# Cross attention's mask as a table that VectorE adds to the scores, in place of a TensorE matmul, on one core

## The reference

```python
kv_c = kv @ W_kvc;  q_c = q @ W_dq                     # q = layernorm(x), kv = ctx_2048 (16, 1601, 256)
q_nope, q_rope = heads(q_c @ W_uq), rope(heads(q_c @ W_qr))        # 16 heads of 128, of 64
k_nope, v, k_rope = heads(kv_c @ W_uk), heads(kv_c @ W_uv), rope(kv_c @ W_kr)
scores = (q_nope . k_nope + q_rope . k_rope) / sqrt(192)
good = (k_ids <= seg_id) & (k_ids >= seg_id - 8)       # seg_id: one number per query token, 0 to 127
attn = softmax(where(good, scores, -1e30))             # over the 1601 keys
x = x + (attn @ v) @ W_o
```

## Time and profile before

| | us |
|---|---|
| median of 3 runs | 519.15 |
| lowest, highest | 518.19, 522.25 |
| the profiled execution: its time | 518.47 |
| the profiled execution: its span | 516.7 |
| PE busy | 499.3 (97%) |
| PEld busy | 363.5 (70%) |
| DVE busy | 249.6 (48%) |
| ACT busy | 185.2 (36%) |

### The profile page before, as it was taken

How to read it: one execution, slowest core, us unless ns; L and a number is a source line. 1 busy time by engine, 2 the same in 40 slices (tenths; PEclk the granted TensorE clock), 3 DMA queues, 4 the chain that set the end, 5 groups by cost and what they waited for, 6 DMA issues and landing times.

```text
span 516.7 us, 10575 instructions
## 1 busy us (share of the span) xinstructions
PE 499.3 (97%) x3878; PEld 363.5 (70%) x3878; DVE 249.6 (48%) x549; ACT 185.2 (36%) x534; POOL 60.3 (12%) x71
## 2 busy tenths in 40 slices
PE   8699999999999999997999998999999999999997
PEld 7476777777877788885798885555555555556886
DVE  2565876876766668987553221222222222222334
ACT  2157567566566444444411111112112112121110
POOL 2000000000000122132006500000000000000650
PEclk9799999999999999999999999999999999999999
DMA  9800000000991009400523162777877877852241
GB/s 289 321 22 1 20 22 1 19 20 15 362 410 48 2 17 408 189 0 1 209 98 126 70 220 90 269 264 279 306 270 283 310 261 291 301 210 82 80 125 41
DMA packets 24455, 82.05 MB, mean 159 GB/s; under 512 B 2880, under 2 KB 16512, under 8 KB 20320
## 3 DMA queue, kind: packets, MB, share of 16 engines
q1 hardware_dynamic: 21536, 75.93, 40.3%
q0 software_dynamic: 1536, 4.20, 2.6%
q10 hardware_dynamic: 1344, 1.38, 0.8%
HBM read 73.10 MB, written 8.39 MB: 158 GB/s over the span
## 4 chain that ended last, share of the span: by engine, by line
PE 88%; DVE 6%; issue 3%; ACT 2%; POOL 0%; DVEq 0%; ACTq 0%; POOLq 0%
PE ps L1808 17%; PE ps L1721 12%; PE ps L1317 12%; PE ps L1832 9%; PE ps L1733 6%; PE ps L1396 5%; PE ps L1346 5%; PE ps L1365 5%; PE ps L1488 3%; PE ps L1384 3%; ACT w_routed L1096 1%; PE ps L1322 1%; PE ps L1498 1%; PE ps L1677 1%; PE ps L1338 1%
## 5 line engine op out<-in xcount | busy, mean ns | idle before, releaser
L1808 PE MATMUL ps<-w_routed,xnT 128*64 x320 | 93.8, 436 | 1.6 <-DVE x_sb L967 1.6
L1721 PE MATMUL ps<-xT_all,w_shared 128*128 128x256 f32 x320 | 75.7, 380 | 0.0
L1808 PEld LDWEIGHTS ps<-w_routed,xnT 128*64 128x64 f32 x320 | 42.0, 137 | 38.4 <-issue 27.2
L1721 PEld LDWEIGHTS ps<-xT_all,w_shared 128*128 128x128 f32 x320 | 60.3, 190 | 8.4 <-issue 0.4
L1096 ACT ACTIVATE w_routed<-ps,neg_top 128x128 f32<-128x128 f32 x128 | 45.1, 379 | 15.8 <-DVE neg_top L637 15.8
L1317 PEld LDWEIGHTS ps<-consts_a,w_routed 128*128 128x128 f32 x336 | 38.8, 145 | 15.2 <-issue 12.1
L1317 PE MATMUL ps<-consts_a,w_routed 128*128 128x128 f32 x336 | 46.2, 283 | 2.4 <-DVE x_sb L565 1.4
L1832 PE MATMUL ps<-w_routed,hidT 128*64 x200 | 47.4, 384 | 0.0
L1808 PE MATMUL ps<-w_shared,xnT 128*64 128x384 f32 (+1 forms) x160 | 46.9, 436 | 0.0
L1808 PE MATMUL ps<-x_up,xnT 128*64 128x384 f32 (+1 forms) x160 | 46.9, 436 | 0.0
L1286 ACT COPY hidT<-ps 128x384 f32<-128x384 f32 x20 | 9.6, 479 | 100.7 <-PE ps L1317 100.7
(11 more groups left out here) (181 smaller groups left out, 870.6 us busy)
## 6 DMA issues: line engine op xcount, KB each, us to landing
w_routed<-in_w_routed SPq DMA_DIRECT2D x8, 1920.0 KB, 14.4
x_up<-in_w_routed SPq DMA_DIRECT2D x10, 1280.0 KB, 5.9
w_shared<-in_w_routed SPq DMA_DIRECT2D x10, 1280.0 KB, 6.1
b_down<-in_w_routed SPq DMA_DIRECT2D x10, 640.0 KB, 5.7
w_shared<-in_w_routed SPq DMA_DIRECT2D x10, 640.0 KB, 5.4
w_shared<-in_w_shared SPq DMA_DIRECT2D x1, 3840.0 KB, 11.7
w_shared<-in_w_uvo SPq DMA_DIRECT2D x1, 2560.0 KB, 15.4
x_slots<-sil SPq DMA_DIRECT2D x16, 160.0 KB, 2.1
```

The lines of the kernel that those rows point to most:

```text
L1721: last = pe.matmul(ps[:, UP_BANK[m], half_ * D:(half_ + 1) * D].rearrange("p (n t) -> p n t", n=2), w_shared[:, j, at:at + P], xT_all[:, i ...
L1808: last = pe.matmul(ps[rows, b, 0:hi - lo], xnT[:, k, rows], w, start=k == 0, stop=k == KT - 1)
```

## The change

In the setup, behind the first tile's queries, TensorE runs four matmuls of `sel` with the mask of four tiles each (512 columns, banks 4 to 7), and ScalarE copies each result as bf16 into a table `spread` of 128 x (8 tiles, 2 sequences, 128 keys), which lies in `b_down`, unused until the experts. In each tile the mask's four matmuls go, and a bank's score matmuls each start afresh. VectorE adds the table's row block, repeated over the four head pairs, to the scores in PSUM and writes them to `Pb` in SBUF (with a `link`), and takes the minimum from there. ScalarE's exponentials read `Pb` in place of PSUM, in place. The general path keeps its matmul and waits for the table.

```diff
+        spread = b_down[:, 0:NT * TB * P // 2].bitcast(BF16).rearrange("p (n b t) -> p n b t", n=NT, b=TB)
...
@@ general
+                eng.wait_ge(spread_done, 2 * TB)
...
@@ vector
-            def maxima(i, b):
+            def maxima(i, b, link_):
                 s = scores_at(b)
                 for g in range(2):
                     n = slice(4 * g, 4 * g + 4)
                     dve.wait_ge(s_ps, 2 * TB * i + 2 * b + g + 1)
-                    dve.tensor_reduce(neg_top[:, b, n], s[:, n], AX.X, ALU.min).then_inc(top_ready, 1)
+                    link_(dve.tensor_tensor(Pb[:, b, n], s[:, n], spread[:, i, b, :].unsqueeze(1).to_broadcast([P, 4, P]), ALU.add))
+                    dve.tensor_reduce(neg_top[:, b, n], Pb[:, b, n], AX.X, ALU.min).then_inc(top_ready, 1)
...
+            dve.wait_ge(spread_done, 2 * TB)
             body(0, link, False, True)
             body(1, link, True, True)
             base = steps[0]
-            K = 8
+            K = 12
...
@@ scalar
             def exps(i, b, groups=(0, 1)):
-                s = ps[:, 4 + 2 * b:6 + 2 * b, :].rearrange("p r (h t) -> p (r h) t", t=P)
                 for g in groups:
                     act.wait_ge(top_ready, 2 * TB * i + 2 * b + g + 1)
                     for n in range(4 * g, 4 * g + 4):
-                        last = act.activation(Pb[:, b, n, :], s[:, n, :], ACT.Exp, scale=-1.0,
+                        last = act.activation(Pb[:, b, n, :], Pb[:, b, n, :], ACT.Exp, scale=-1.0,
                                               bias=neg_top[:, b, n:n + 1], accum_out=sums[:, b, n:n + 1])
...
             lat_out(0)
+            for n in range(2 * TB):
+                act.wait_ge(spread_ps, n + 1)
+                act.copy(spread[:, n // TB * NT // 2:(n // TB + 1) * NT // 2, n % TB, :],
+                         ps[:, 4 + n, :].rearrange("p (n t) -> p n t", t=P)).then_inc(spread_done, 1)
...
@@ tensor
-            def scores_work(b, half_, window):
+            def scores_work(b, half_, window=None):
                 at = ps[:, 4 + 2 * b + half_, :]
-                pe.matmul(at.rearrange("p (n k) -> p n k", k=P), sel[:, b, :], window.unsqueeze(1).to_broadcast([P, 4, P]),
-                          start=True, stop=False)
+                if window is not None:
+                    pe.matmul(at.rearrange("p (n k) -> p n k", k=P), sel[:, b, :], window.unsqueeze(1).to_broadcast([P, 4, P]),
+                              start=True, stop=False)
                 for n in range(4):
                     h = 2 * (4 * half_ + n)
-                    last = pe.matmul(at[:, n * P:(n + 1) * P], QT[:, b, h:h + 2, :], KTb[:, b, :], start=False, stop=n == 3)
+                    last = pe.matmul(at[:, n * P:(n + 1) * P], QT[:, b, h:h + 2, :], KTb[:, b, :], start=window is None,
+                                     stop=window is None or n == 3)
...
             y_rope(0)
+            pe.wait_ge(win_ready, 1)
+            pe.wait_ge(far_ready, 1)
+            for n in range(2 * TB):
+                pe.matmul(ps[:, 4 + n, :].rearrange("p (n t) -> p n t", t=P), sel[:, n % TB, :],
+                          win[:, n // TB * NT // 2:(n // TB + 1) * NT // 2, :], start=True, stop=True).then_inc(spread_ps, 1)
...
-            pe.wait_ge(win_ready, 1)
+            pe.wait_ge(spread_done, 2 * TB)
             body(0, False)
```

More of the change, by code:

```diff
@@ L282, in build @@
             yrope_ps yrope_used qrope krope kT_ps kT_done qt_lo_ps qt_lo qt_hi_ps qt_hi kvx
-            s_ps top_ready exp_done p_done pt_ps pt_done ut_ps ut_done proj_ps x2_done ones_set
+            s_ps top_ready exp_done spread_ps spread_done p_done pt_ps pt_done ut_ps ut_done proj_ps x2_done ones_set
             bxn bT_ps bxT_done bq_ps bqm bkv_ps bk_done bv_done bs_ps bs_used bmax bsub bp_done bpt_ps
@@ L291, in build @@
          yrope_ps, yrope_used, qrope, krope, kT_ps, kT_done, qt_lo_ps, qt_lo, qt_hi_ps, qt_hi, kvx,
-         s_ps, top_ready, exp_done, p_done, pt_ps, pt_done, ut_ps, ut_done, proj_ps, x2_done, ones_set,
+         s_ps, top_ready, exp_done, spread_ps, spread_done, p_done, pt_ps, pt_done, ut_ps, ut_done, proj_ps, x2_done, ones_set,
          bxn, bT_ps, bxT_done, bq_ps, bqm, bkv_ps, bk_done, bv_done, bs_ps, bs_used, bmax, bsub, bp_done, bpt_ps,
@@ L675, in last_body @@
                 normed(0, 5, xn, bT_ps, bxn, 0)
-                maxima(i, 0)
+                maxima(i, 0, link_)
                 divided(i, 0, link_)
                 b_queries(0)
-                maxima(i, 1)
+                maxima(i, 1, link_)
                 normed(1, 7, xn, bT_ps, bxn, 1)
@@ L1438, in scores @@
                 after(pe, ut_done, TB * i - 1 + b)
-                scores_work(b, 0, win[:, i, :]).then_inc(s_ps, 1)
+                scores_work(b, 0).then_inc(s_ps, 1)
                 pe.wait_ge(qt_hi, i + 1)
@@ L1442, in scores @@
                     after(pe, x2_done, i - 1)
-                scores_work(b, 1, win[:, i, :]).then_inc(s_ps, 1)
+                scores_work(b, 1).then_inc(s_ps, 1)
             def probs_T(i, b):
```

## The result

The changed kernel takes 524.71 us (median of 7 runs, 522.98 to 525.9) against 519.17 for the kernel before (7 runs): ratio 1.0097, 95% interval 1.0078 to 1.0117. It is slower by 1%, 3.8 us above the forecast and inside its range. The profiled execution took 523.71, its span 521.9, 5.2 longer than before.

The account below looks back on a forecast made before the run. TensorE was taken as the bound, VectorE following at 72%. For the profiled execution 518.47 + 0.3 (setup) + 1.35 (tile 0) - 0.9 - 0.3 (middle tiles) + 1.3 (last tile) = 520.2; median forecast 520.9 us, range 515.5 to 525.5.

Parts of the forecast that it names:

- the very string that the forecast added up: Cross attention tile: addition, maximum, exponentials, reciprocal, twice, plus VectorE's work between; 18.73 us against TensorE's 18.02.
- Rival 3: Cross attention: VectorE's added work is hidden and TensorE stays the bound; 513.4 us, chance 0.05.
- the halves: Each half's addition 0.71 with its wait, maximum 0.69, then 2.94 to the reciprocal, plus 0.28 for dearer exponentials.
- rivals 1 and 2: Exponentials reading SBUF: 1, the full 74 ns extra each, 525.9 us, chance 0.17; 2, no cost, some 517.4, chance 0.13.
- a tile gains 0.15, six tiles 0.9, and tile 6 perhaps 0.3 more: Middle tiles: VectorE's loop of 18.17, with ScalarE's 0.56 18.73, just under 18.88; tile 6 has no statistics to make.
- the loop that I had called 0.1 shorter: Second loop per tile: ScalarE's keys' copy behind the exponentials holds the query transposes, then TensorE's 4.2 to the next maximum.
- Tile 0: First tile, without cover: both halves' additions and exponentials lengthen TensorE's wait for ScalarE's keys; +1.35 us.
- The last tile: Last tile, where TensorE already waits for the divided probabilities: +1.2 us, charged 1.3 for an extra ScalarE copy.
- Setup: Four matmuls in TensorE's idle 4.76 and four covered ScalarE copies; +0.3 charged for the skipped general path's branch.
- rival 4: Setup's branch: ScalarE, after its copies, spends as long on it as TensorE; 2.2 to 2.5 more, 523.3 us, chance 0.12.
- rival 5: Setup: TensorE's idle shortened to 3.9 might keep the clock from falling; 2.3 won, 518.6 us, chance 0.05.
- Nothing gives it back behind cross attention: Behind cross attention TensorE is 97% busy too, so nothing there gives the added time back.

Follow-up runs that it names:

- e1_no_mask: The kernel before without its 32 mask matmuls and nothing in their place (mask left out): 516.83 us, ratio 0.9954.
- e2_both: The changed kernel with TensorE's mask matmuls kept as well, so the mask is added twice: 526.45 us, ratio 1.0159.
- e4_in_psum: The changed kernel with the sum written back over the scores in PSUM, read there by maxima and exponentials; complete: 520.86 us, ratio 1.0048.
- e3_exp_psum: The changed kernel with exponentials reading the unmasked scores in PSUM, addition and maximum kept: 520.28 us, ratio 1.0021.
- e5_after_unrolled: The changed kernel with VectorE's loop over tiles 2 to 5 written out: 523.16 us, ratio 1.0092.
- e10_in_psum_unrolled: The changed kernel with the sum written back over the scores in PSUM and VectorE's loop written out: 519.53 us, ratio 1.0007.
- e12_rotate_pool: The changed kernel with sum in PSUM, VectorE's loop written out and the queries' rotation sum made by GpSimd: 518.79 us, ratio 0.9996.
- e8_half: The changed kernel with TensorE masking the first head halves, VectorE only the second, sum in SBUF: 518.34 us, ratio 0.9995.
- e9_half_psum: The changed kernel with TensorE masking the first head halves, VectorE the second, sum written back in PSUM: 518.37 us, ratio 0.9982.
- e7_before_exp_sbuf: The kernel before with cross attention's exponentials reading a constant SBUF tile instead of the scores (values wrong): 521.07 us, ratio 1.0041.

## Why the prediction was right, and where it was off

**Right: direction and mechanism.** TensorE's 0.86 a tile is real (0.85 in e1_no_mask), and it is not had, since a string through VectorE and ScalarE takes over (0.07 in e2_both's middle tiles). It is the very string that the forecast added up: the chain that ended last runs along it in the tile shown, and a saving on its exponentials arrives in full (e4_in_psum). Rival 3 is out. The size was off: +1.75 forecast for the profiled execution, +5.2 measured.

**Right: the halves.** From addition to reciprocal 4.67 and 4.66, forecast 4.64. In it the exponentials cost 0.041 each (0.385 against 0.344), where I took 35 ns between 0 and 74; rivals 1 and 2 are out. The Trainium skill's "VectorE: DVE Perf Modes", section "The TRN2 errata", from which I had worked out 43 ns as an estimate, is borne out by this better than my pair of rows was.

**Wrong: the middle tiles' size and sign,** the step "a tile gains 0.15, six tiles 0.9, and tile 6 perhaps 0.3 more", out of the sum 8.72 + 5.07 + 4.65 - 0.27, with ScalarE's 0.56 18.73. They lost 2.2, and this error of 3.4 is as large as the whole miss. The terms in the tile shown:

- from the first reciprocal to the second half's addition 5.17 (92.14 to 97.31), forecast 5.07 - 0.09 = 4.98: 0.19 more. The wait before line 598 was taken off whole, and 0.11 of it stayed (line 614 ends at 94.87, line 600 starts at 94.98). What line 600 waits for are the rotary queries; TensorE starts their second half 0.55 late for the raw keys, and ScalarE's copy of these stands behind the first half's exponentials. So the result awaited moved with the work put in;
- from the second reciprocal to the next first addition 4.91 (101.97 to 106.88), forecast 4.65 - 0.18 = 4.47: 0.44 more. This is the turn of VectorE's loop, 0.36 from line 569's end (106.52) to the addition, and the 0.09 of overlap that I had credited. Before, the turn lay under the wait of 1.04; with that gone it shows. It is 0.36 in e3_exp_psum and e4_in_psum too, though there the scores start only 1.27 and 1.25 ahead of the addition and not 1.38. Written out, 0.29 of the period goes (e5_after_unrolled);
- the two halves 0.03 and 0.02 more. Together 0.68, the whole of 19.41 - 18.73.

Close behind lies the loop that I had called 0.1 shorter, through the scores: 19.12 in e5_after_unrolled, 0.29 less. The scores hang on the query transposes, and these not only on ScalarE's keys, as I had it, but also on VectorE's rotation sum, which stands behind the second half's additions and maxima in its queue. That branch through line 627 I did not add up, though its row at 96.24 stood in the earlier trace rows. Its reader, in the order of time of the kernel before:

```profile
99.11 1.91 PE L1317 MATMUL ps<-consts_a,w_routed 128*128 128x128 f32 x16
```

That is 1.65 behind the sum's end (96.24 + 1.22). The change puts one addition and the dearer exponentials of the first half (0.71 + 0.28) and both additions of the second (1.42) ahead of the sum, 2.41 in all. Of this 1.72 arrives there (11.97 from the first maximum to the sum's end before, 13.69 from the first addition now), most of the rest going into the wait before line 598; it is still more than the 1.65. e10_in_psum_unrolled and e12_rotate_pool show this branch as the one that holds once the exponentials and the loop's turn are shortened, but not that it sets the changed kernel's 19.41.

That the total fell inside the range is partly luck: against the middle tiles' 3.4 and 1.0 more in tile 0 and behind cross attention stands a setup that came out 0.95 better than forecast.

**Tile 0** +1.78, forecast +1.35. The wait came where it was expected, before the transposes, but for VectorE's rotation sum and not for ScalarE's keys (tile 0, order of time):

```profile
41.74 2.10 PE L1324 MATMUL ps<-consts_a,w_routed 128*128 128x128 f32 x16 [1.47 <-DVE w_routed L627]
```

**The last tile** +1.28, forecast +1.3.

**Setup** -0.65, forecast +0.3 within -2.3 to +2.5. Order of time, on TensorE and on ScalarE, and the stretch of the earlier trace rows:

```profile
22.44 0.66 PE L1324 MATMUL ps<-consts_a,hidT 128*128 128x128 f32 x2 [3.77 <-issue]
...
22.89 3.10 PE L1324 MATMUL ps<-consts_a,w_routed 128*128 128x128 f32 x16
```

```profile
23.14 0.38 ACT L1084 ACTIVATE hid<-ps 128x256 f32<-128x256 f32 x1 [3.02 <-PE ps L1324]
```

```profile
24.70:27.00 2.30, 1.80 (x14) 1.59 (x13) 1.54 (x2) 0.97 (x2) 0.00 (x0) 0.87 0.00 0
```

TensorE comes back at 22.44 as before at 22.49, so its wait shrank by what was put ahead of it, and ScalarE is ready when the keys are: rival 4 is out. Of rival 5 a part came: the clock was still low at first but rose earlier (0.87 for 0.50).

**Nothing gives it back behind cross attention**: so it was for a loss (+0.6). For a gain it is otherwise, as e1_no_mask shows; had rival 3 come true, its 513.4 would have been some 516.8.

## What to carry to other kernels

Before counting an engine's wait as room for new work, ask two things. First, follow the awaited result back: if it comes, over other engines, from the same queue that the new work goes into, the wait moves along and hides less than its length (here the rotary queries, through ScalarE's raw keys; and the query transposes, whose slack of 1.65 us met 1.72 more). Second, ask what of the engine's own lay under the wait: the turn of VectorE's loop, 0.36 us, cost nothing while it waited 1.04 and everything once the wait was gone. Splitting the work so that half of it falls under another engine's stretch (e8_half, e9_half_psum) got what moving all of it could not.

## What was not expected of the hardware

Executions of one kernel differ by whether the granted clock falls to its lower level for a stretch: in e1_no_mask eight matmuls took 2.93 and 2.83 in place of 1.89, in e7_before_exp_sbuf 3.21. The changed kernel took 525.15 and 525.9 at mean clock 0.990 and 522.98 at 0.996, but also 524.71 at 0.997, so the clock is not all of it. VectorE's first addition comes 0.36 behind the instruction before it where the loop turns between them; the maximum of the kernel before stands 1.09 behind its scores in its loop too, from 84.40 to 85.49 in the earlier trace rows, since there VectorE waits. How much of the 0.36 is the loop's branch and how much the counter in the addition's operand and waits was not separated. GpSimd needed 2.34 us for a sum of 128x1024 that took VectorE 1.22, and VectorE's addition beside it kept its 0.69.
